# Places of the side work in attention slots: one table for each of four kinds of slot, both halves of Gelu in one stay of ScalarE, and gathers two parts ahead in the expert stage

## The reference

```python
for i in range(NL):                                   # NL = 6, B = 4
    xn = _adaln(x, noise_emb, n1_w[i], n1_b[i])
    q, k, v = split(xn @ qkv_w[i].T); q, k = rope(q), rope(k)
    x = x + attn(q, k, v) @ so_w[i].T
    xn = _adaln(x, noise_emb, n2_w[i], n2_b[i])
    q = rope(xn @ cq_w[i].T); k = rope(context @ ck_w[i].T); v = context @ cv_w[i].T
    x = x + attn(q, k, v) @ co_w[i].T
    xn = _adaln(x, noise_emb, n3_w[i], n3_b[i])
    h = gelu(xn @ f1_w[i].T + f1_b[i]); x = x + (h @ f2_w[i].T + f2_b[i])
```

## Time and profile before

| what | value |
|---|---|
| median of 3 runs | 4456.39 us (4449.91 to 4459.43) |
| profiled execution, its own time | 4442.28 us |
| its span | 4440.6 us |
| PE, DVE, ACT, POOL busy (page, part 1) | 3940.5, 2907.1, 2561.9, 857.7 us |

### The profile page before, as it was taken

The page is one execution under the profiler, slowest core; times in us unless marked ns, Lnnn a source line. Parts: engine busy times, 40 slices in busy tenths (PEclk is TensorE's granted clock), DMA queues, the critical chain, the costliest instruction groups (busy, mean ns, idle before and its releaser), DMA issues. The chain is left out here.

```text
span 4440.6 us, 68492 instructions
## 1 busy us (share of the span) xinstructions
PE 3940.5 (89%) x20630; PEld 1833.7 (41%) x20630; DVE 2907.1 (65%) x4711; ACT 2561.9 (58%) x4302; POOL 857.7 (19%) x518
## 2 busy tenths in 40 slices
PE   3699999999999999999999999999999999997467
PEld 1233344533344533345433345433345433354355
DVE  3777766677766678766678766678766677752311
ACT  1376656667666567666567665567666566654122
POOL 4312121112121112211111211111211121200133
PEclk7799999999999999999999999999999999999689
DMA  5354323244323244332244332244332344410234
GB/s 162 85 135 108 97 69 78 63 108 120 87 78 72 60 113 119 87 80 65 67 108 116 94 72 66 68 108 116 97 75 59 74 129 111 109 30 13 83 99 95
DMA packets 271578, 396.39 MB, mean 89 GB/s; under 512 B 28312, under 2 KB 218400, under 8 KB 270880
## 3 DMA queue, kind: packets, MB, share of 16 engines
q1 hardware_dynamic: 263904, 382.18, 34.1%
q0 software_dynamic: 7296, 9.51, 1.3%
HBM read 226.63 MB, written 170.67 MB: 89 GB/s over the span
## 5 line engine op out<-in xcount | busy, mean ns | idle before, releaser
L837 ACT ACTIVATE prob<-ps 128x512 f32<-128x512 f32 x3072 | 1768.2, 596 | 1225.2 <-PE ps L761 1207.6
L999 DVE TENSOR_REDUCE negmax<-ps 128x2 f32<-128x1024 f32 x1536 | 1836.7, 1219 | 217.6 <-PE ps L788 195.2
L761 PE MATMUL ps<-qstack,kstack 114*128 114x512 bf16 x3072 | 1162.4, 389 | 100.1 <-ACT prob L837 84.8
L774 PE MATMUL psv<-prob,v 128*32 128x512 f32 x6144 | 829.5, 612 | 0.0
L761 PEld LDWEIGHTS ps<-qstack,kstack 114*128 114x128 bf16 x3072 | 284.6, 97 | 1190.3 <-ACT prob L837 794.5
L616 POOL TENSOR_TENSOR rot<-ropep 128x512 f32<-128x512 f32 x96 | 122.5, 1276 | 2486.7 <-DVE ropep L1032 2467.7
L788 PE MATMUL ps<-kstack,qstack 49*128 49x512 bf16 x3072 | 496.8, 388 | 97.9 <-DVE negmax L999 76.8
L736 PE MATMUL side<-anat,wf 128*128 128x256 f32 x1536 | 377.1, 388 | 9.9 <-DVE hT L1037 8.9
L1037 DVE TENSOR_SCALAR hT<-side,f1b 128x256 f32<-128x256 f32 x384 | 168.2, 479 | 303.6 <-PE side L736 303.6
L747 PE MATMUL side<-wf,hT 128*128 128x256 f32 x1536 | 347.9, 379 | 2.8 <-DVE x L1044 1.6
L736 PEld LDWEIGHTS side<-anat,wf 128*128 128x128 f32 x1536 | 285.6, 192 | 65.7 <-DVE hT L1037 30.9
(11 more groups left out here) (158 smaller groups left out, 3722.1 us busy)
## 6 DMA issues: line engine op xcount, KB each, us to landing
bounce<-parts SPq DMA_DIRECT2D x480, 256.0 KB, 2.5
qstack<-bounce SPq DMA_DIRECT2D x384, 192.0 KB, 5.5
kstack<-bounce SPq DMA_DIRECT2D x384, 192.0 KB, 6.1
bounce<-low SPq DMA_DIRECT2D x96, 256.0 KB, 2.1
ctxT<-in_ctxT SPq DMA_DIRECT2D x24, 512.0 KB, 3.9
nw<-in_nwT SPq DMA_DIRECT2D x18, 512.0 KB, 11.3
w<-in_w SPq DMA_DIRECT2D x16, 512.0 KB, 4.8
wself<-in_wself SPq DMA_DIRECT2D x24, 256.0 KB, 4.0
```

The costliest lines, as they stand in the source:

```text
L761: nc.tensor.matmul(ps2[:, n % RING2, :], kk[0:ROWS, h, kt * P:(kt + 1) * P], q[0:ROWS, h, :], start=True, stop=True).then_inc(s_p2full, 1)
L774: mm = nc.tensor.matmul(psv[32 * i:32 * i + 32, 0, :], v[j % 2][:, kt, (HD + 1) * h:(HD + 1) * h + 32], prob[:, 4 * (u % 2) + i, :], start ...
L837: nc.scalar.activation(prob[:, 4 * (u % 2) + i, :], ps2[:, n % RING2, :], ACT.Exp, scale=HD ** -0.5).then_inc(s_prob, 1)
L999: nc.vector.tensor_reduce(out_at, ps1[:, 2 * (n % 2):2 * (n % 2) + 2, :], AX, ALU.max, negate=True).then_inc(s_p1free, 1)
```

## The change

Five things are changed.

1. The two tables become four: short slots, short slots after a long one (also slots 0 to 2), long slots, and long slots after a long one. Many side chunks stand a place or two elsewhere: in short slots HQ and HK are at places 9, 11, 13, 15 (were 9, 10, 12, 14); in long slots O and T2 come ahead of HT, LT is at 16 and 18 (were 17 and 18) with HK at 15 and 17, and F2 begins at 28 (was 27).
2. The layer norm for HT moves from the first places of a slot to places 22 to 28 of the short slot before it (`LN_NEXT`); after a long slot it stays at the start (`LN_HT`).
3. DVE reduces both pairs of a unit before it reads a chunk of HQ, HK, O, F1 or F2 at the even place (`both`). The first `shift_parts` goes from behind maximum 17 to behind maximum 16.
4. Both halves of Gelu stand at place 26, with one table load ahead and one behind (were at 23 and 27, with two each).
5. In `experts`, `gather_T` and `read_T` go one part further ahead of `hidden`.

```diff
-SHORT_PLACES = {
-    "HV": [1, 3], "T1": [2, 4, 5, 7], "HT": [6, 8], "HQ": [9, 10], "HK": [12, 14],
-    "T2": [15, 17], "O": [19, 21],
...
+SHORT = {
+    "M": [23, 0], "HV": [1, 3], "T1": [2, 4, 6, 8], "HT": [5, 7], "HQ": [9, 11], "HK": [13, 15],
+    "T2": [16, 18], "O": [19, 21], "SPLIT": (13, 15, 19, 21),
+    "LN_NEXT": dict(stats=[22, 22, 23, 23], aggregate=24, guess=25, newton=26, tiles=[27, 27, 28, 28]),
...
+LONG = {
+    "M": [29, 0], "HV": [1, 3], "T1": [2, 4, 5, 6], "T2": [7, 8], "O": [9, 10], "HT": [11, 12], "HQ": [13, 14],
+    "HK": [15, 17], "LT": [16, 18], "F1": [19, 20, 21, 22, 23, 24, 25, 26], "F2": [28, 29, 30, 31],
+    "SPLIT": (16, 18, 20, 22), "GELU": 26,
+    "LN_LT": dict(stats=[10, 10, 10, 10], aggregate=11, guess=12, newton=13, tiles=[13, 14, 14, 15]),
...
-            def gelu(k, th):
-
-                wait_read(act, place, k, "F1", 4 * th + 3)
-                nc.scalar.activation(hT[th][:, :, :], hT[th][:, :, :], ACT.Gelu).then_inc(s_gelu, 1)
+            def gelu(k):
+
+
+                for th in range(2):
+                    wait_read(act, place, k, "F1", 4 * th + 3)
+                    nc.scalar.activation(hT[th][:, :, :], hT[th][:, :, :], ACT.Gelu).then_inc(s_gelu, 1)
                 act.preload_act_table_set(EXP_SET)
...
-                    if p1:
+
+                    both = any(what in ("HQ", "HK", "O", "F1", "F2") for what, c in plan[2 * u])
+                    if p1 and half == 0:
                         maximum(k, at)
-                        if at == 17:
-                            shift_parts(k, 0)
+                        if both:
+                            maximum(k, at + 1)
+                    if p1 and half == 1 and not both:
+                        maximum(k, at)
+                    if p1 and at == 16:
+                        shift_parts(k, 0)
...
+
             gather_T(0)
             hidden(0)
+            gather_T(1)
             for n in range(len(PARTS)):
                 if n + 1 < len(PARTS):
-                    gather_T(n + 1)
                     hidden(n + 1)
+                if n + 2 < len(PARTS):
+                    gather_T(n + 2)
                 outputs(n)
```

More of the change, by code:

```diff
@@ L394, in is_ffn, with places_of, norm_steps @@
             return k >= 2 and is_cross(k - 2)
+        def places_of(k):
+            after_long = k < 2 or is_ffn(k - 1) or k == 2
+            return ((SHORT, SHORT_AFTER_LONG), (LONG, LONG_AFTER_LONG))[is_ffn(k)][after_long]
+        def norm_steps(k):
+            steps, places = [], places_of(k)
+            if "LN_HT" in places and k + 1 < 2 * NJ:
+                steps.append((k, "HT", places["LN_HT"]))
+            if "LN_LT" in places:
+                steps.append((k, "LT", places["LN_LT"]))
+            if "LN_NEXT" in places and "LN_HT" not in places_of(k + 1) and k + 2 < 2 * NJ:
+                steps.append((k + 1, "HT", places["LN_NEXT"]))
+            return steps
         def slot_chunks(k):
@@ L917, in slot @@
                 ffn = is_ffn(k)
-                splits = LONG_SPLIT if ffn else SHORT_SPLIT
+                places = places_of(k)
+                splits = places["SPLIT"]
                 for at in range(2 * SLOT_UNITS):
@@ L930, in slot @@
                         side_work(k, what, c)
[L931 to L934, removed]
+                    for of, what, steps in norm_steps(k):
+                        if at == steps["guess"]:
+                            rstd_guess(of, what)
                     if head and at in splits:
@@ L937, in slot @@
                         (hi, mid)[step](k + 1, n)
-                    if ffn and at in GELU_PLACES:
-                        gelu(k, GELU_PLACES.index(at))
+                    if ffn and at == places["GELU"]:
+                        gelu(k)
             run_slots(act, place, head0, slot)
@@ L962, in stats @@
                         wait_read(dve, place, k, "O", 1)
+                    elif "LN_HT" not in places_of(k):
+                        wait_read(dve, place, k - 1, "O", 1)
                     elif steps[0]:
@@ L1068, in slot @@
                 plan = slot_chunks(k)
-                ffn = is_ffn(k)
                 for at in range(2 * SLOT_UNITS):
                     u, half = divmod(at, 2)
-                    if p1:
+                    both = any(what in ("HQ", "HK", "O", "F1", "F2") for what, c in plan[2 * u])
+                    if p1 and half == 0:
                         maximum(k, at)
-                        if at == 17:
-                            shift_parts(k, 0)
+                        if both:
[4 more added lines that the diff above has]
+                        shift_parts(k, 0)
                     for what, c in plan[at]:
                         side_work(k, what, c)
[L1078 to L1081, removed]
+                    for of, what, norm in norm_steps(k):
                         for t in range(TT):
-                            if at == places["stats"][t]:
-                                stats(k, what, t)
-                        if at == places["aggregate"]:
+                            if at == norm["stats"][t]:
+                                stats(of, what, t)
+                        if at == norm["aggregate"]:
                             aggregate(what)
-                        if at == places["newton"]:
-                            normalise(k, what)
+                        if at == norm["newton"]:
+                            normalise(of, what)
                         for t in range(TT):
-                            if at == places["tiles"][t]:
-                                normed(k, what, t)
+                            if at == norm["tiles"][t]:
+                                normed(of, what, t)
                 if p1:
```

35 lines of the change are left out of this document (15 added, 20 removed).

## The result

The changed kernel takes 4617.43 us (median of 4 runs, 4604.32 to 4620.18), the kernel before beside it 4455.45 (4449.91 to 4459.43): a ratio of 1.0361, with an interval of 1.0344 to 1.0378. I had said 4422 and at most 4475. The profiled execution took 4619.52, its span is 4617.8; the spans differ by 177.2 us.

What follows compares the result with a forecast made beforehand. PE's own stream was taken to bound the kernel. Short slots -45, long slots +29 and experts -18 gave -34 us, stated as 4422 us on the median of 4456.4; range over all cases 4355 to 4475.

Steps and rivals of the forecast that it cites:

- the price of a unit: PE's timeline: a bare unit takes 2.7 us without a gap, an F1 chunk 1.83 us.
- The Gelu pause, term 4.4: Long slots, unit 14's pass two: PE pauses 4.4 us behind the Gelu pair; net +3.1 us a slot.
- The clock, +1.5 for the new pause: Long slots: 1.2 GHz after each Gelu pause costs 1.5 us; 1.0 of earlier loss goes, net +0.5.
- the clock outweighs all: Rival, units 14 and 15: clock loss after Gelu makes the kernel slower, about 4482 us at 4 a slot; 17%.
- (d): Short slots: shift_parts ahead of unit 8's second reduction, and ACT's HT copies at odd places, cost 0.8 us.
- put 1.2 on the slot: First slot of a layer: norm at both ends, split of k a unit later; taken as -1.2 us, 6 slots.
- Terms (a) to (c): Short slots: reduction waits in units 5 to 7 -2.3 us, Exp waits -1.4, norm in units 11 to 15 +0.8.
- my 2.1: Short slots: the net gain forecast per slot, -2.3 - 1.4 + 0.8 + 0.8 = -2.1 us, for 18 slots.
- (a): Short slots, units 5 to 7: waits for the second reduction and the bank go, -2.3 us.
- the rival that it binds: Rival, units 11 to 15 of short slots: the tail norm costs 2.5 us, not 0.8, so no change; 16%.
- Long slots without Gelu, -2.4: Long slots: waits at HQ, HK and LT fall, HK and LT to 1.3 us each; -2.4 a slot, bounds 0 and -5.5.
- Experts, -18: Expert stage: PE's waits for DVE's copy of gathered rows go, -18 us; bounds 0 and -20.

Runs made afterwards that it cites:

- the pair alone: The kernel before with both Gelu halves at place 26 under one table load and F2 at 28 to 31: 4607.74 us, ratio 1.0349.
- the mended kernel: The changed kernel with first shift_parts behind maximum 17, Gelu halves at 23 and 27, shift rows sent ahead of stack loads: 4377.82 us, ratio 0.9829.
- the pair of reductions alone: The kernel before with both reductions of a unit ahead of reading an even-place chunk, shift_parts still behind maximum 17: 4465.08 us, ratio 1.0028.
- the fastest version: The mended kernel with long slots' M at 27 and HQ's even chunk read between the two reductions there: 4336.92 us, ratio 0.9751.

## Why the prediction was wrong

- **Which engine bounds, and the price of a unit: right.** Every difference was found in PE's waits and the clock behind them, and no busy time decided one.
- **The Gelu pause, term 4.4: right** (4.2 in the row), and so was its place and that nothing fills it. Gelu starts 1.29 us behind the start of its table load here too (1396.77 to 1398.06), and the whole stay takes 6.31 us. The Trainium skill, page "ScalarE: Activation LUTs", section "What ACT_TABLE_LOAD costs", counts 1.38 us for a drain at each switch besides; the trace does not agree.
- **The clock, +1.5 for the new pause: too small.** It is 2.4 by the changed kernel's rows and up to 3.2 by the pair alone. I took a size seen behind a pause of 2.6 for one of 4.4, though my own rows had slots with a loss of 2.5. The clock falls in every long slot, as I said. The rival "the clock outweighs all" has the right sign and a part of the mechanism: behind the Gelu pause, 0.9 to 1.7 us more in 22 slots is 20 to 37 of the 196 us between forecast and outcome. What it missed, and I too, is that the clock falls behind the new waits of the short slots and of slots 2 as well, where I had put it at nothing; by the estimate above that is some 60 us more, and it is contained in the terms (d) and SP's queue below. Even so the clock only follows waits that have other causes: without the three waits, in the mended kernel, it is 25 us of PE's work.
- **The M chunk, missed: 0.8 a long slot.** I counted F2's move to 28 and not that M now stands directly ahead of a chunk in the same bank. With M at 27 the mended kernel gained 19 us.
- **Term (d), 0.8 for `shift_parts` and HT: the first step that failed.** I gave the move no row and no wait of its own. Beside POOL's work the three operations take 2.6 us, and pass one waits 2.1 of it for the reduction behind them; the kernel before had shown 2.4 for them at a place where nothing waited. Undone, it gave 77 us, in short slots and slots 2, where I had counted 24 x 0.8 = 19 with the HT copies.
- **SP's queue, missed: the second step that failed.** I wrote that in slots 2 the split of k ends a unit later and put 1.2 on the slot without following the loads of that split into the queue, where the shift rows stand behind them. The waits are 46 us, and with the rows sent first the kernel gained 59, 10 of it in the head.
- **Terms (a) to (c): right in sign, too good in size.** Short slots of the mended kernel take 64.5, 1.9 less than before. That is near my 2.1 by luck: the 2.1 has the 0.8 of (d) in it, and most of (d) is undone there, so up to 2.9 should have come. Of (a), 2.3, the pair of reductions alone gave 1.3. The norm in the tail is worth some 12 us against the norm at the start, so the rival that it binds did not come true.
- **Long slots without Gelu, -2.4: too good.** LT waits 1.4 and HK 0.8, where my working had 1.3 each, and the wait at LT fell from 2.6; but both reductions ahead of HQ cost much of it again. Taken back for HQ alone, that gave 22 us, 1.1 a slot.
- **Experts, -18: right in mechanism, too small in size.** Alone the part gave -25, beyond my bound of -20. The -17.7 between the two traces look like a hit by luck: the last two long slots, with their Gelu pause, lie in that stretch.

Put together: between forecast and outcome lie 196 us (-34 and +162, the latter between the medians). Of these, (d) is 77 - 19 = 58 and the queue 59, each with the clock behind its waits, M 19, and the clock behind the Gelu pause about 26. What remains, 34, would be 1.5 in each of the 22 long slots, by which -2.4 was too good. That last number is what is left over. An estimate from the version with M at 27 agrees with it: its long slots are 0.45 us shorter than before, by -1.0 for the clock, +1.4 for the wait behind the second Gelu (2.5 for 1.1) and so some -0.85 for the order, against -2.4. The terms are medians and good to about 10 us each, and the queue's 59 hold the 10 of the head, where the change lost nothing; so the split of the 196 is rougher than its digits.

## What to carry to other kernels

An operation that is moved is to be costed by its row beside what the other engines do, not by its mean, and then ask who waits for what now stands behind it: 2.4 us of VectorE cost nothing behind both reductions, and 2.6 ahead of one cost 77 us in all. Where VectorE and GpSimd both work from SBUF, look at GpSimd's timeline there. Where a step ends later, follow every transfer that waits for it, and ask which small, urgent ones stand behind it in the same queue; sending the small ones first cost three waits of 1.0 to 1.7 us here and gave 59. To save two table loads on an engine that isn't waited for, by a longer hold-up of the one that is, lost 158 us: count the longest hold-up, and the clock behind it, before the number of loads. The same goes for every new wait: here the clock fell even behind one of 2.1 us.

## What the hardware showed that I had not expected

- A cast of 128 x 32 took 1.18 us and a subtraction 1.20 beside two operations of 128 x 512 on POOL, six times their 0.17 and 0.19, and each ended with POOL's; the kernel before has casts of 1.06 and 1.14 there. The Trainium skill, page "SBUF — State Buffer", section "Who interferes with whom", says that such operations of VectorE and GpSimd take one port pair in turns and that the later one blocks until the first ends; by that rule, the trace agrees.
- TensorE's clock was at 0.50 already in the pause of 4.2 us, and stayed there for some 4.9 us of work behind it.
- At each of the four jumps back of the loop VectorE stood for 4.3 to 5.9 us in the kernel before, and for 5.1 to 5.9 in the fastest version, without a wait that the profile names. The cause is open; no run here tried one.
